# One softmax normalisation and one set of row statistics moved in VectorE's instruction order of a gated cross-attention and expert layer

## The reference, cut to what matters

```python
# B = 32 batches, N = 256 rows, width 256; context 77 rows of 512; 16 heads of 64
x = x + tanh(g_xattn) * xattn(layernorm(x), ctx)
x = x + tanh(g_ffn) * ffn(layernorm(x))

def xattn(x, context):
    q = heads(x @ Wq) * 64 ** -0.5
    k, v = heads(split(context @ Wkv))          # a null key and a null value are put in front
    attn = softmax(q @ k.T, axis=-1)            # 78 columns
    out = merge(attn @ v) @ Wout
    return (out - mean(out)) * rsqrt(var(out) + 1e-6) * ln_scale + ln_bias

def ffn(x):                                     # 8192 rows, 32 experts, 8 picked for each row
    aff = sigmoid(x @ Wr + br)
    w_full = weights of the 8 largest, divided by their sum; 0 elsewhere
    shared = (silu(x @ Wg_s + bg_s) * (x @ Wu_s + bu_s)) @ Wd_s + bd_s
    return shared + sum over e of w_full[:, e] * expert_e(x)
```

## Time and profile before

| | before |
|---|---|
| median of 3 runs | 2383.68 us (2380.78 to 2391.0) |
| the profiled execution | 2380.78 us, span 2379.0 us |
| TensorE busy | 2091.6 us (88%) |
| VectorE busy | 1835.1 us (77%) |
| ScalarE busy | 1528.1 us (64%) |
| GpSimd busy | 1313.4 us (55%) |
| granted TensorE clock, mean | 0.959 of full |

### The profile page before, as it was taken

One profiled execution on the slowest core, in us unless ns is written; L12 is line 12 of the kernel. 1 busy time (PEld: TensorE's weight loads), 2 busy tenths in 40 slices (PEclk: granted clock), 3 DMA queues, 4 the chain that ended last, 5 costly groups with the idle time before them and its releaser, 6 DMA issues. The chain is left out here.

```text
span 2379.0 us, 44646 instructions
## 1 busy us (share of the span) xinstructions
PE 2091.6 (88%) x14418; PEld 1919.3 (81%) x14418; DVE 1835.1 (77%) x4294; ACT 1528.1 (64%) x4487; POOL 1313.4 (55%) x1444
## 2 busy tenths in 40 slices
PE   7999678999999999999995789999988998989982
PEld 6888578888988888888995678888877887778772
DVE  4544357888888888888886668778988998989884
ACT  4433346776777676667763238888776777767761
POOL 1000214777777777777775600005777777767766
PEclk9999789999999999999997899999998999999996
DMA  8987489987788878787884999999999999999995
GB/s 274 329 288 262 135 287 315 309 263 255 262 268 269 269 263 265 256 266 253 270 271 174 333 388 303 300 297 357 373 369 344 371 376 360 378 349 366 369 343 161
DMA packets 385523, 710.02 MB, mean 298 GB/s; under 512 B 136427, under 2 KB 249036, under 8 KB 382828
## 3 DMA queue, kind: packets, MB, share of 16 engines
q1 hardware_dynamic: 336140, 564.50, 68.9%
q0 software_dynamic: 49152, 142.67, 17.3%
HBM read 349.16 MB, written 357.83 MB: 297 GB/s over the span
## 5 line engine op out<-in xcount | busy, mean ns | idle before, releaser
L1459 POOL DMA_INDIRECT parts<-results_dram,kept_index x512 | 543.7, 1062 | 464.4 <-DMA results_dram<-y 262.6
L771 POOL DMA_INDIRECT pages_dram<-rows,kept_index x472 | 474.1, 1004 | 132.9 <-issue 121.1
L840 ACT ACTIVATE exps<-sim,minus_max 128x78 f32<-128x78 f32 x1024 | 318.5, 356 | 32.7 <-DVE minus_max L918 31.0
L1510 ACT ACTIVATE hid_h<-hidden 128x512 fp32r<-128x512 f32 x176 | 111.2, 632 | 237.5 <-DVE hidden L1605 234.2
L1489 ACT ACTIVATE y<-yps,row_weight 128x256 f32<-128x256 f32 x640 | 248.1, 470 | 2.2 <-PE yps L132 2.2
L840 ACT ACTIVATION_READ_ACCUMULATOR exps<-sim,minus_max 128x1 f32 x1024 | 242.6, 238 | 0.0
L1658 PE MATMUL xps<-ident,xin 128*128 128x128 f32 x1280 | 173.6, 280 | 74.9 <-DVE wq_l L1529 46.5
L1658 PEld LDWEIGHTS xps<-ident,xin 128*128 128x128 f32 x1280 | 144.1, 144 | 89.1 <-issue 88.3
L130 PE MATMUL yps<-w_h,hid_h 128*128 128x256 f32 x640 | 181.1, 283 | 2.0 <-ACT y L1489 2.0
L131 PE MATMUL yps<-w_h,hid_l 128*128 128x256 f32 x640 | 181.5, 284 | 0.0
L132 PE MATMUL yps<-w_l,hid_h 128*128 128x256 f32 x640 | 181.0, 283 | 0.0
(11 more groups left out here) (268 smaller groups left out, 7566.5 us busy)
## 6 DMA issues: line engine op xcount, KB each, us to landing
xin<-pages_dram SPq DMA_DIRECT2D x160, 576.0 KB, 6.7
results_dram<-y SPq DMA_DIRECT2D x160, 512.0 KB, 5.2
pages_dram<-blank SPq DMA_DIRECT2D x108, 576.0 KB, 9.0
w_raw<-in_experts SPq DMA_DIRECT2D x160, 385.0 KB, 5.5
pages_dram<-blank SPq DMA_DIRECT2D x12, 1728.0 KB, 13.3
keys_h_dram<-keys_h SPq DMA_DIRECT2D x32, 624.0 KB, 5.7
keys_l_dram<-keys_l SPq DMA_DIRECT2D x32, 624.0 KB, 7.6
kT_h<-keys_h_dram SPq DMA_DIRECT2D x32, 624.0 KB, 5.7
```

The costliest lines, as they stand in the source:

```text
L771: pool.indirect_dma_start(dram["pages"], bass.IndirectOffsetOnAxis(ap=kept_index[:, at:at + 1].bitcast(U32), axis=0), buffer(batch)[:, k / ...
L840: last = act.activation(exps[u % 2][:, h, :], scores(u)[:, h // 4, h % 4, :], ACT.Exp, bias=minus_max[u][:, h:h + 1], accum_out=row_sum[u] ...
L1459: pool.indirect_dma_start(parts[t][:, k, :], None, done, bass.IndirectOffsetOnAxis(ap=kept_index[:, at:at + 1].bitcast(U32), axis=0)).then ...
L1510: act.activation(hid[s % 2][0][:, :], hidden[s % 2][:, :], ACT.Copy).then_inc(hid_hi, 1)
```

## The change

In iteration `b`, VectorE does three things at other places:

- `normalise(3, b)` is no longer between the evictions of Q1 and PV0a but between those of PV0a and PV0b.
- `statistics(2, ...)` of batch `b-1`, with its wait for GpSimd's `summed`, is no longer behind the eviction of T3b but behind that of T3a, ahead of Q2's.
- The routing steps "opened" are done behind T3a as well, ahead of those statistics.

Nothing is added or taken away, and the lists of the other engines stay as they were.

```diff
--- before.py
+++ after.py
@@ -97,7 +97,7 @@
 LAST_PICKS = 8
 
 
-ROUTE_AFTER = {"T1a": ["logits", "top", "mask"], "PV0b": ["placed"], "T3a": ["affinity"], "T3b": ["opened", "page", "moved"],
+ROUTE_AFTER = {"T1a": ["logits", "top", "mask"], "PV0b": ["placed"], "T3a": ["affinity", "opened"], "T3b": ["page", "moved"],
                "Q3": ["slot"], "PV1a": ["key"], "PV1b": ["weight"]}
 
 ROUTE = ["biased", "logits", "top", "without_top", "mask", "placed", "next_end", "divisor", "affinity", "picked", "total",
@@ -1074,9 +1074,6 @@
                     maximum(3, b)
                 for name in EVICTED if b >= -1 else ():
                     low(name, b)
-                    if name == "T3b" and 1 <= b <= B:
-                        dve.wait_ge(summed, b)
-                        statistics(2, lambda t: x1[1 - par][:, t, :], b - 1)
                     if name == "T0a" and 1 <= b <= B:
                         dve.wait_ge(ring_full, nth(RING, "Ob", b))
                         statistics(1, lambda t: bank("Ob")[:, t * D:(t + 1) * D], b - 1)
@@ -1085,8 +1082,11 @@
                             route(part, b, par, h)
                     if name == "T1b" and here:
                         normalise(2, b)
-                    if name == "Q1" and here:
+                    if name == "PV0a" and here:
                         normalise(3, b)
+                    if name == "T3a" and 1 <= b <= B:
+                        dve.wait_ge(summed, b)
+                        statistics(2, lambda t: x1[1 - par][:, t, :], b - 1)
                     if name == "Q3" and b <= B - 3:
                         dve.wait_ge(x_loaded, 16 * (b + 3))
                         statistics(0, lambda t: x_in[:, t, :], b + 2)
```

## The result

The changed kernel takes 2421.32 us in the median of 4 runs (2415.34 to 2421.62), the one before 2387.34 (2380.78 to 2391.24). The ratio is 1.0149 with a 95% interval of 1.0130 to 1.0169: slower by about 34 us. The profiled execution took 2423.91 us, 43 more than that of before, which happened to be the fastest of before's four runs. The forecast was slower by about 22 us, 2405, with a range of its own of 2395 to 2416. The direction and the place are right and the size is too small.

What follows compares the result with a forecast made beforehand. A loop through VectorE, GpSimd's shift, `xn`, X and the similarities was taken to set the period. 30.05 + 1.05 = 31.10, up to 31.4, against the mean 30.51 over 28 iterations gave +22 us: 2405, range 2395 to 2416.

Steps and rivals of the forecast that it cites:

- The loop through VectorE, `xn`, X and the similarities: Attention phase: this loop sets the 30.05 us period; a microsecond more on VectorE is a microsecond more of period.
- Part 1, the wait: VectorE after Q1, with normalise(3) moved: it waits for PV0a's high half, 1.17 us of idle time that was filled.
- Part 1, the collision: Unit 3's normalisation beside GpSimd: the collision moves from L798 to L801, L933 about 1.3 us, L801 about 1.6.
- slip: Unit 3's normalisation: L933 gets in ahead of L801, so PV0b's low half comes with no loss.
- The forecast's third case: Unit 3's normalisation: VectorE comes 0.2 us later, L932 waits for all of L801, delay about 1.3 us.
- Part 1, the delay: PV0b's low half starts 1.05 us later, bounds 0 and 1.3; period 31.10, up to 31.4 us.
- Part 2, hidden by the slack before X: Statistics(2) and "opened" ahead of Q2's eviction: uses up TensorE's 1.35 us before X, costs about 0.1 us by itself.
- The wait for `summed`: VectorE behind T3a's eviction: costs nothing, since L801 ends at 806.4 and VectorE arrives at 810.2.
- the sum: Attention phase: new period against the mean of 30.51, +0.6 to +0.9 us over 28 iterations, +17 to +25, taken as +22.
- Rival C: TensorE before T3a and PV1a: half-clock stretches in every second iteration, 18 us on top of 22, 2424 us; chance 0.15.
- The seven double collisions: Iterations after a half-clock stretch, where GpSimd hits both normalise(3) multiplications, 1.79 and 1.33 us; taken as in the mean already.
- Rivals A and B: A: all iterations 30.05 us, 2371, chance 0.12. B: L933 slips in or `z` comes earlier, no change, 2384, chance 0.18.

Runs made afterwards that it cites:

- e5: The kernel before with one more GpSimd scatter issued ahead of L798: 2376.78 us against 2386.61, ratio 0.9962.
- e2b: The changed kernel with `normalise(3, b)` back behind Q1, so only statistics(2) and "opened" moved: 2398.25 us, ratio 1.0044 to the kernel before.
- The filled kernel: The changed kernel with extra overwritten matmuls, 10 before T3a and 8 before PV1a: 2412.01 us against 2386.61 of the kernel before, ratio 1.0109.

## Why the prediction was right in kind and wrong in size

- **What bounds the kernel.** The loop through VectorE, `xn`, X and the similarities was the right one to look at: what part 1 adds to VectorE appears in the period. But e5 shows that it is not a loop of VectorE alone. From Q1 to T3a, ScalarE and TensorE are within half a microsecond of it.
- **Part 1, the wait.** 1.17 us of idle time was forecast, 1.11 measured.
- **Part 1, the collision.** Forecast: it moves from L798 to L801, L933 at 1.3 and L801 at 1.6. Measured: 1.33 and 1.69. No slip was seen. The forecast's third case came as well, behind the twelve stretches: L932 waits for all of L801, 1.60 us, and PV0b's low half starts 4.40 us behind `z` (891.10 - 886.70), 1.32 later than before, where about 1.3 was given. The Trainium skill's page "SBUF — State Buffer" (section "SBUF: two separate sides") has an exclusive lock between a VectorE operation with two SBUF inputs and a GpSimd one that reads SBUF, held for the whole instruction by the one that starts first. Both forms agree with it.
- **Part 1, the delay.** PV0b's low half starts 4.24 us behind `z` (1212.61 - 1208.37), where it was 3.08 (805.43 - 802.35), so 1.16 later instead of 1.05. T3a's eviction ends 1.23 later, the statistics of `x_in` 1.39 later (1221.42 against 814.01, each from its `z`). The forecast carried 1.05 through the rest of the iteration unchanged. It left out that T3a's high half now comes after the normalisation and that "opened" right behind the last affinity step has to wait for it (0.25 us from that step's start, where Q2's eviction stood 0.13 behind it). The quiet period of 31.43 us is at the upper end of the 31.10 to 31.4 that were given. TensorE's idle time is 1.44 us before T3a and 2.08 before PV1a, where 1.3 and 1.8 were forecast.
- **Part 2, hidden by the slack before X.** Right in a quiet iteration: 0.17 us by e2b, and X without idle time. The wait for `summed` cost nothing, as said.
- **The step that failed** is the sentence in the sum that the "double collisions and the clock drops are in the mean already and the new place is hit every time anyway". The sum is the quiet period after less the mean of before. So it took off what stretches and double collisions cost before, 0.46 us an iteration (30.51 - 30.05), 13 us in all, and put in nothing for the half-clock stretches after. The runs showed 20 of them where before had 4, and 0.59 us an iteration (32.02 - 31.43), 17 us in all. The filled kernel, without stretches, shows the same term: 0.52. Rival C had their mechanism and place and was given a chance of 0.15 as something apart, where it was a term of the likeliest case. Its time, 2424, came nearest to the measured 2421, by luck in part: it had 10 further stretches at 1.8 us each, and there were 16, at 0.7 in the mean over all 20. It also took before's drops for one in every fourth iteration; the steady part has 4 in 26. The forecast had worked out that part 2 collects 1.8 us of idle time in one place, more than the 1.35 before X that preceded the drops of before, and that was reason enough to put the stretches into the sum.
- **The sizes.** Between the profiled executions: the quiet period (31.43 - 30.51) x 28 = 26 us, the stretches (32.02 - 31.43) x 28 = 17, together 43. The forecast had 22 and 0. Between the medians it is 34, because before's profiled execution was 7 us faster than its median and that of the changed kernel 3 us slower than its own.
- **The seven double collisions** of the sum are those of the whole phase. In the 26 periods over which the mean of 30.51 is taken there are five.
- **Rivals A and B** fell with L933 at 1.33 us and z rows no less than 31.4 apart.

What stays open: how the 1.38 us of the quiet period split between the wait for ScalarE and the collision. No undisturbed run took the collision out of the changed kernel.

## What to carry to other kernels

A step of work that fills a wait on one engine is free where it stands. Before moving it, ask what its old place was waiting for and what its new place collides with; here both answers could be read from neighbouring iterations of the trace. Idle time of TensorE is not neutral when it moves: collected in longer pieces it brought more half-clock stretches here, and just ahead of work with no slack each of them was paid in full. These belong into the sum of the likeliest case. When a forecast takes the mean of before as its base, what that mean holds beyond the quiet period has to be estimated for after as well. And a collision that takes 1.1 us of an instruction is worth only what the next engine's result would have allowed, here 0.23.

## What the runs showed of the hardware

- TensorE's clock fell to 1.2 GHz within iterations whose idle pieces were 1.4 and 2.1 us (2.16 was the longest in the steady part), and stayed at 2.4 GHz through 26 iterations once 18 matmuls an iteration, about 2.5 us of overwritten work, had cut these pieces to 0.2 and 1.1 us. Useless work made the kernel about 9 us faster (2421.32 to 2412.01).
- The granted clock fell after the idle piece, in work that runs without a gap (0.50 from 866.3 to 869.6 us), and the price hung on what came next: 0.8 to 1.0 us where X followed without slack, 0 to 0.4 where TensorE's wait before PV1a stood in between.
- Two operations of VectorE and two of GpSimd that met went in turn, and both sides lost: L798, then L932, then L801, which took 1.69 us instead of 1.27, then L933, which took 1.33 instead of 0.27.
